# Last feed-forward of a four-layer network: tiles turned by DMA instead of TensorE, and both silus ahead of the older tile's rounding

## What is computed

```python
def _weight_quant(w):
    scale = 1.0 / jnp.clip(jnp.mean(jnp.abs(w)), 1e-05)
    wq = jnp.clip(jnp.round(w * scale), -1.0, 1.0) / scale
...
def _act_quant(x):
    scale = 127.0 / jnp.clip(jnp.max(jnp.abs(x), axis=-1, keepdims=True), 1e-05)
    xq = jnp.clip(jnp.round(x * scale), -128.0, 127.0) / scale
...
def _bitlinear(x, w):
    return jnp.einsum('bsi,oi->bso', _act_quant(x), _weight_quant(w))
gate = jax.nn.silu(_bitlinear(x, w_gate))
up = _bitlinear(x, w_up)
return _bitlinear(gate * up, w_down)
```

## Time and profile before

| | |
|---|---|
| time, 3 runs | 1109.73 us median, 1107.92 to 1112.27 |
| the profiled execution's own time | 1105.96 us |
| its span, first to last instruction | 1104.2 us |
| last feed-forward in the span | 992.7 to 1104.2 us |
| first matmul of its rounds | 1020.77 us |
| TensorE, VectorE, ScalarE, POOL busy over the span | 83%, 71%, 68%, 56% |
| mean granted TensorE clock | 0.934 |

### The profile page before, as it was taken

The page is one execution under the profiler, slowest core; times in us unless marked ns, Lnnn a source line. Parts: engine busy times, 40 slices in busy tenths (PEclk is TensorE's granted clock), DMA queues, the critical chain, the costliest instruction groups (busy, mean ns, idle before and its releaser), DMA issues. The chain is left out here.

```text
span 1104.2 us, 23943 instructions
## 1 busy us (share of the span) xinstructions
PE 914.9 (83%) x9014; PEld 698.9 (63%) x9014; DVE 782.2 (71%) x1550; ACT 745.7 (68%) x1254; POOL 623.5 (56%) x571
## 2 busy tenths in 40 slices
PE   5887998999999999997518999967888989960686
PEld 4655686767676777675417999955566767760344
DVE  5768778777877786676894444458978786639676
ACT  3387888698878887882533444445797878924686
POOL 2177766776686666772515555333686767813232
PEclk9899999999999999998758999988998999975899
DMA  9479999899989979994912222182899979943011
GB/s 265 164 127 193 160 157 152 153 171 151 163 145 184 158 149 152 149 175 65 321 67 73 77 75 75 58 282 43 173 187 173 168 145 172 173 78 114 6 35 39
DMA packets 433744, 153.57 MB, mean 139 GB/s; under 512 B 406592, under 2 KB 424192, under 8 KB 433600
## 3 DMA queue, kind: packets, MB, share of 16 engines
q1 hardware_dynamic: 429888, 141.82, 66.6%
q0 software_dynamic: 3744, 10.23, 2.9%
HBM read 38.62 MB, written 12.71 MB: 46 GB/s over the span
## 5 line engine op out<-in xcount | busy, mean ns | idle before, releaser
L477 POOL TENSOR_TENSOR A_PHL<-A_pr,A_PHL 128x508 f16<-128x508 f32 x256 | 295.2, 1159 | 134.5 <-ACT A_pr L754 133.6
L753 ACT ACTIVATE A_PHL<-A_ps,A_negmax 128x508 f16<-128x508 f32 x256 | 179.6, 701 | 17.9 <-DVE A_negmax L1003 15.3
L477 POOL TENSOR_TENSOR C_PHL<-C_pr,C_PHL 128x512 f16<-128x512 f32 x128 | 150.5, 1186 | 58.0 <-ACT C_pr L754 57.5
L754 ACT ACTIVATE A_pr<-A_ps,A_negmax 128x508 f32<-128x508 f32 x256 | 181.5, 709 | 0.0
L1003 DVE TENSOR_REDUCE A_negmax<-A_ps 128x2 f32<-128x1016 f32 x128 | 154.3, 1205 | 0.0
L598 PE MATMUL A_ps<-A_K,A_Q 64*128 64x512 f32 x768 | 124.1, 427 | 12.4 <-ACT A_pr L754 9.8
L616 PE MATMUL A_ps<-A_VH,A_PT 128*128 128x65 bf16 (+1 forms) x1024 | 109.5, 197 | 18.9 <-DMA A_PT<-A_PHL 18.6
L616 PEld LDWEIGHTS A_ps<-A_VH,A_PT 128*128 128x128 f16 (+1 forms) x1024 | 93.6, 98 | 47.7 <-DMA A_PT<-A_PHL 29.6
L617 PE MATMUL A_ps<-A_VL,A_PT 128*128 128x64 f16 (+1 forms) x1024 | 108.6, 194 | 0.0
L618 PE MATMUL A_ps<-A_VH,A_PT 128*128 128x65 bf16 (+1 forms) x1024 | 108.3, 195 | 0.0
L753 ACT ACTIVATE C_PHL<-C_ps,C_negmax 128x512 f16<-128x512 f32 x128 | 88.7, 693 | 15.1 <-DVE C_negmax L1003 14.5
(11 more groups left out here) (355 smaller groups left out, 2681.8 us busy)
## 6 DMA issues: line engine op xcount, KB each, us to landing
A_PT<-A_PHL SPq DMA_TRANSPOSE x256, 3.4
M_WINl<-in_L_ffn_w_in SPq DMA_DIRECT2D x4, 1024.0 KB, 11.9
M_WOUTl<-in_L_ffn_w_out SPq DMA_DIRECT2D x4, 1024.0 KB, 12.5
C_yc<-routed_rows SPq DMA_DIRECT2D x8, 512.0 KB, 5.2
ct_split<-A_CT SPq DMA_DIRECT2D x4, 768.0 KB, 4.1
C_CT<-ct_split SPq DMA_DIRECT2D x4, 768.0 KB, 8.0
M_rows<-M_xn SPq DMA_DIRECT2D x4, 512.0 KB, 9.0
out<-X SPq DMA_DIRECT2D x16, 128.0 KB, 1.7
```

The costliest lines, as they stand in the source:

```text
L477: pool.tensor_tensor(PHL[:, e % PRING, 1, 0:KEYS], pr[:, e % RING, 0:KEYS], PHL[:, e % PRING, 0, 0:KEYS], ALU.subtract).then_inc(pl_ready. ...
L753: a.activation(PHL[:, e % PRING, 0, 0:KEYS], o, ACT.Exp, bias=nm[:, n % 4, h:h + 1])
L754: a.activation(pr[:, e % RING, 0:KEYS], o, ACT.Exp, bias=nm[:, n % 4, h:h + 1]).then_inc(p_ready.sem, 1)
```

## The change

Input tiles and inner tiles are transposed by DMA, issued from SP, straight from SBUF to SBUF. TensorE's transposes and ScalarE's two copies go. The PSUM that they used becomes a third buffer of F_pg (GU = 3) and a second of F_py. F_xqT, F_hq and F_hqT get three buffers, and LAG, the rounds between a tile's start and its down product, goes from 3 to 4. On ScalarE silu(s, 1) moves ahead of h_round(s - 1). The three weight-load semaphores are shared with the attention's.

```diff
-    LAG = 3
+    LAG = 4
     XLEAD = 2
-    HB = 4
+    HB, HQ, XQ, GU = 4, 3, 3, 3
...
+            def turn_x(t):
+                sp.wait_ge(xq_ready, t // GRP + 1)
+                if t >= XQ:
+                    sp.wait_ge(gu_filled, 2 * (t - XQ + 1))
+                sp.dma_start_transpose(out=xqT[:, t % XQ, :, :], in_=xq[:, t // GRP % 2, t % GRP, :]).then_inc(xt_loaded[t % XQ], 16)
+
+            def turn_h(t):
+                sp.wait_ge(hq_ready, t + 1)
+                if t >= HQ:
+                    sp.wait_ge(y_filled, t - HQ + 1)
+                sp.dma_start_transpose(out=hqT[:, t % HQ, :, :], in_=hq[:, t % HQ, :]).then_inc(ht_loaded[t % HQ], 16)
+
+            def store(t):
                 sp.wait_ge(x_added, t + 1)
                 sp.dma_start(out[:, t, :], X[:, t, :]).then_inc(stored, 16)
+
+            for t in range(XLEAD):
+                turn_x(t)
+            for s in range(NT + LAG + 2):
+                if s + XLEAD < NT:
+                    turn_x(s + XLEAD)
+                if 2 <= s < NT + 2:
+                    turn_h(s - 2)
+                if s >= LAG + 2:
+                    store(s - LAG - 2)
...
             def gate_up(t, half):
                 u = 2 * t + half
                 if half == 0:
-                    pe.wait_ge(xt_copied, t + 1)
-                if u >= 2:
-                    pe.wait_ge(h_ready, u - 1)
+                    pe.wait_ge(xt_loaded[t % XQ], 16 * (t // XQ + 1))
+                if u >= GU:
+                    pe.wait_ge(h_ready, u - GU + 1)
...
+            def down(t):
+                pe.wait_ge(ht_loaded[t % HQ], 16 * (t // HQ + 1))
                 if t >= 2:
-                    pe.wait_ge(ht_copied, t - 1)
+                    pe.wait_ge(x_added, t - 1)
...
             for s in range(NT + LAG):
                 if s < NT:
                     silu(s, 0)
+                    silu(s, 1)
                 if 1 <= s <= NT:
                     h_round(s - 1)
-                if s < NT:
-                    silu(s, 1)
-                if LAG - 1 <= s < NT + LAG - 1:
-                    h_copy(s - LAG + 1)
-                if s + XLEAD < NT:
-                    x_copy(s + XLEAD)
```

More of the change, by code:

```diff
@@ L1638, in bit_ffn @@
         hs = sb("hs", [P, 2, H], F32)
-        hq = sb("hq", [P, 2, H], BF16)
-        hqT = sb("hqT", [P, 2, HC, P], BF16)
-        w_loaded = [sem(f"w_loaded{k}") for k in range(3)]
+        hq = sb("hq", [P, HQ, H], BF16)
+        hqT = sb("hqT", [P, HQ, HC, P], BF16)
+        w_loaded = [turn_of(stats, "attn", nc, f"w_{n}_loaded", 16) for n in "qkv"]
         chain_sem = sem("chain")
@@ L1654, in bit_ffn @@
         xq_ready = sem("xq_ready")
-        xt_filled = sem("xt_filled")
-        xt_copied = sem("xt_copied")
+        xt_loaded = [sem(f"xt_loaded{k}") for k in range(XQ)]
         gu_filled = sem("gu_filled")
@@ L1663, in bit_ffn @@
         hq_ready = sem("hq_ready")
-        ht_filled = sem("ht_filled")
-        ht_copied = sem("ht_copied")
+        ht_loaded = [sem(f"ht_loaded{k}") for k in range(HQ)]
         y_filled = sem("y_filled")
@@ L1685, in _ @@
             pe.wait_ge(sums_ready, 2)
[L1686 to L1695, removed]
+            mm(py[:, 0, 0:4], ones[:, :], wsum[:, :], start=True, stop=True).then_inc(sums_filled, 1)
             def gate_up(t, half):
@@ L1699, in gate_up @@
                 if half == 0:
-                    pe.wait_ge(xt_copied, t + 1)
-                if u >= 2:
-                    pe.wait_ge(h_ready, u - 1)
+                    pe.wait_ge(xt_loaded[t % XQ], 16 * (t // XQ + 1))
+                if u >= GU:
+                    pe.wait_ge(h_ready, u - GU + 1)
                 for j, W in enumerate((WG, WU)):
                     for kc in range(KC):
-                        last = mm(pg[:, half, j, :], xqT[:, t % 2, kc, :], W[:, kc, half * BANK:(half + 1) * BANK],
+                        last = mm(pg[:, u % GU, j, :], xqT[:, t % XQ, kc, :], W[:, kc, half * BANK:(half + 1) * BANK],
                                   start=(kc == 0), stop=(kc == KC - 1))
                 last.then_inc(gu_filled, 1)
-            def turn_h(t):
-                pe.wait_ge(hq_ready, t + 1)
+            def down(t):
+                pe.wait_ge(ht_loaded[t % HQ], 16 * (t // HQ + 1))
                 if t >= 2:
-                    pe.wait_ge(ht_copied, t - 1)
+                    pe.wait_ge(x_added, t - 1)
                 for c in range(HC):
[L1714 to L1722, removed]
+                    last = mm(py[:, t % 2, 0:D], hqT[:, t % HQ, c, :], WD[:, c, :], start=(c == 0), stop=(c == HC - 1))
                 last.then_inc(y_filled, 1)
-            for t in range(XLEAD):
-                turn_x(t)
             pe.wait_ge(w_ready, 3)
@@ L1749, in x_final @@
                 if g >= 2:
-                    pool.wait_ge(xt_filled, GRP * (g - 1))
+                    for t in range(GRP * (g - 2), GRP * (g - 1)):
+                        pool.wait_ge(xt_loaded[t % XQ], 16 * (t // XQ + 1))
                 pool.tensor_scalar(xq[:, g % 2, :, :], xr[:, g % 2, :, :], -MAGIC, 1.0, ALU.add, ALU.mult).then_inc(xq_ready, 1)
@@ L1784, in x_round @@
                              scale=xm[:, 1, t:t + 1]).then_inc(x_rounded, 1)
[L1786 to L1790, removed]
             for t in range(2 * GRP):
```

49 lines of the change are left out of this document (17 added, 32 removed).

## The result

The changed kernel takes 1095.35 us (median of 11 runs, 1091.27 to 1102.74), the kernel before, timed beside it, 1109.24 (11 runs, 1104.75 to 1113.45). The ratio is 0.988, with an interval of 0.9856 to 0.9904: 13.3 us less, give or take 2.7.

What follows compares the result with a forecast made beforehand. A closed 4.18 us loop through ScalarE and VectorE was taken as the bound, falling to 3.50. Loop -10.5 and end +1.9 gave -8.6 us: profiled 1105.96 to 1097.4, plus 3.8 for the median, 1101.1; range 1097.5 to 1106.0.

Steps and rivals of the forecast that it cites:

- rival 1: The forecast itself: VectorE paces the rounds; 1101.1 us, own range 1098 to 1104.5; chance 0.60.
- Gate to gate, 0.78: VectorE's round: second gate product 0.78 us after the first, part of 3.50 us a round (3.09 without an add).
- The collision, 1.2 us: VectorE's tensor_scalar waits for POOL's group rounding: 0.95 us in round 4, 0.25 in round 8; bounds 0 and 2.1.
- case 2: Larger gain through no collision, short landing and upper clock: 11.2 us, 1098.5 or somewhat less; chance 0.10.
- Moving the second silu is what breaks the loop; removing the transposes is worth nothing by itself.: ScalarE's second silu behind the previous tile's rounding closes the 4.18 us loop; copies and transposes are not on it.
- The end, +1.9: From the last marker to the span's end: 10.7 us in place of 8.8; bounds of the cost 0.5 and 6.0.
- SP: SP's issuing per round: 1.32 + 0.72 and a store, 3.4 us, upper 4.0, against 3.50; costed at nothing.
- The slack of the transposes: In mid-loop, input and inner transposes have over 4 us to spare, even at the 7.7 us maximum landing.
- 3: Long landing at the end, or late input transposes in the first rounds: up to 4.1 us more, 1105.2; chance 0.13.
- 4: Loop not really opened, TensorE's lead only three halves: at 0.5 us more a round, 1109; chance 0.07.
- 5: Transposes do not overlap in the loop: 6.7 us a round, +42 us, 1152; chance 0.05.
- 6: TensorE stays at its lower clock, 1.2 GHz: 5.3 us a round, +14 us, 1124; chance 0.05.

Runs made afterwards that it cites:

- e4: Changed kernel with the small tensor_scalar of each inner tile's scale over two columns in place of one; 1093.81 us, one run.
- e9: Changed kernel with input rounding one round later and scales of four tiles kept in groups of five columns; 1093.2 us, ratio 0.9873 against the kernel before.
- e2: Changed kernel with ScalarE's old order (silu, rounding, silu); 1110.64 us, ratio 1.0018 against the kernel before.
- e1: Kernel before with only both silus moved ahead of the older tile's rounding, TensorE still transposing; 1110.5 us, ratio 1.0019 against the kernel before.
- e7: Changed kernel with the add of the first 11 tiles moved from VectorE to ScalarE and POOL; 1093.59 us, ratio 0.9839 against the kernel before.
- e8: Changed kernel with input rounding one round later and the add of 11 tiles off VectorE; 1093.51 us, ratio 0.9855 against the kernel before.
- e10: Changed kernel with later input rounding, the add of 11 tiles off VectorE and five-column scale groups; 1091.78 us, ratio 0.9874 against the kernel before.
- e11: Changed kernel with later input rounding, the add of 11 tiles off VectorE and fewer scale instructions; 1090.1 us, ratio 0.9828 against the kernel before.
- e3: Changed kernel with two buffers of F_pg in place of three; 1098.42 us, ratio 0.9915 against the kernel before.
- e6: Changed kernel with each inner transpose issued as two DMAs of four blocks; 1106.4 us, ratio 0.9983 against the kernel before.

## Why the prediction was wrong

The sign and the pace-maker were right: VectorE paces the rounds, ScalarE and TensorE follow, nothing waits for a transpose in mid-loop, and the chain is the one of rival 1. The sizes were not: the loop gained 13.8 and not 10.5, and the end cost 1.3 and not 1.9, so the layer fell by 12.4 where I had 8.6. By itself that turns the forecast of 1101.1 into 1097.4, 0.1 below the range. The time, 1095.35, lies 2.15 below the range, and the other 2 us are in no term of mine: the kernel before was 0.5 us faster in 11 runs than in the 3 of the forecast, and 1.5 are within the 2.7 that the gain is uncertain by. Point by point:

**Gate to gate, 0.78 (the step that failed, with the next).** I took the spacing of two gates from the gate and the maximum behind it, since before a wait always parted two gates. Two in a row take 1.40 together (x2 at 1059.68), and the maximum starts 1.43 behind the first (1061.11), where I had charged 1.56. Rounds are 3.36, not 3.50, and 2.95, not 3.09; 15 x 0.14 = 2.1 us. The prediction should have had a bound below 0.78 here; no row of before shows two gates back to back, and I gave this term no range. A sign of it stood in the earlier trace rows. The maximum waits for the result of the gate ahead of it and starts 0.78 behind that gate's start, 0.03 after its 0.75 us are over. The gate behind the add needs nothing of it and starts 0.41 behind its start, 0.07 before its 0.48 us are over. I took the spacing of a pair in which the second waits for the first, and used it for two gates that do not wait for each other; the second of these starts some 0.66 behind the first (1.40 less 0.74), again 0.08 before the first is over. The rows agree with this reading throughout, but no run changes the waiting alone.

**The collision, 1.2 us (the other step that failed).** It did not happen: the 16 instructions L1868 took 0.15 each, the one inside POOL's instruction too. I had drawn the rule from one instruction of 2 columns and applied it to one of 1 column. e4 shows that with 2 columns it costs 0.58 in round 4 and 0.17 in round 8, 0.75 together, so that even there my 0.95 and 0.25 were too much. 2.1 + 1.2 = 3.3, which is the whole of 13.8 - 10.5. My case 2 had the missing collision, at a chance of 0.10, but not the faster gates, and 0 was a bound that I had written down myself, for another reason (a shift in phase).

By the runs, a tensor_scalar of one column is free and those of 2, 4 and 5 wait. I had expected 5 to be free, from 1 against 2 and 4; e9 says no (0.76). The Trainium skill, "VectorE: DVE Perf Modes", section "Mode 2×_2P — use both read ports for one tensor", lets a one-source operation take both read ports when its outermost dimension longer than one is even, or is the same for source and destination. I had read only the first half. With the second, 5 columns in place qualify and one column, which has no such dimension, does not: that rule, read whole, agrees with all four. That the second port is what VectorE waits for is not shown; the runs show only who waits.

**"Moving the second silu is what breaks the loop; removing the transposes is worth nothing by itself."** The second half holds (e2: 1.0018). The first does not: e1 has the move alone and gains nothing either, for a second loop of 4.43 us lies right behind the one of 4.18. I had found the loop that bounds the kernel and not asked which one comes next with the old transposes in place. The number did not suffer, since the change has both.

**The end, +1.9.** My terms add up to 10.6, not the 10.7 that I wrote, so it should have read +1.8. It was +1.3: the landing was 3.1, not 3.6, and the lower clock of the last down product came as worked out (1.89 against 1.87). That clock was a near thing: in e2, e4, e7, e8, e10 and e11 the product ran at the upper clock, 1.05 us, and the end is 0.5 longer than before, which is my lower bound. The runs do not show what decides between the two.

**SP.** The input transpose costs 1.18, not my 0.72; the upper bound, 1.32, was the nearer. The inner one is 1.25 (1.32), the store 0.57 (at most 1.32). What was wrong is the price per block that I had fitted from 8 and 16 blocks; between 2 and 8 blocks the rows differ by 0.07. The sum is 3.0, and 3.24 with the time between one DMA and the next, which I had left out. It stays below the round of 3.36, so that costing it at nothing held, but with 0.12 to spare, and by luck: 0.46 too little for the input transpose and 0.24 left out between the DMAs were made up by 0.75 too much for the store and 0.07 for the inner one. Rounds below 3.24, as in e7, live on the lead of the transposes, and a longer loop would use it up (argued from the two rounds, not run).

**The slack of the transposes.** I wrote that both have over 4 us to spare even at a landing of 7.7. By my own terms that landing leaves the input tile 14 - 1.6 - (2.40 + 1.3 + 7.7) = 1.0 us and the inner one 3.9. No harm came of it, since landings were at most 3.7 and 4.2.

**Start and the rounds with a group maximum.** The start was unchanged, as said (34.3 and 34.5). The two rounds are 6.01 and 5.94, where I had 3.04 + 3.09 = 6.13.

**Rivals.** 3: inner tiles landed in 3.1 us, 4.2 at most, so the end stayed short. 4: e3 takes a third of the lead away and steady rounds stay 3.36, so the lead was ample; only behind the stalls does it matter. 5: transposes overlap, as 3.36 us a round with landings of 2.3 and 3.1 shows; e6 shows where SP's queue does take over. 6: the clock is 1.00 in the steady part, and lower behind the stalls (3.16 us of idle time ahead of 1043.68, where two matmuls take 0.96) and at the end.

## What to carry to other kernels

A loop through several engines has a next-longest loop right behind it: undo each half of a change on its own before crediting one of them. A spacing of two instructions that never stood together in the trace is an unknown and needs bounds like any other; take it from a pair in which the second waits for the first only where that is so in the new order too. A queue's round is read from start to start: the durations of its DMAs alone came to 3.0 us, the round to 3.24. Where an engine has come to pace the rounds (97% busy), every small instruction on it counts in full: 0.4 us of an add (e7) and 0.9 and 1.4 us of small scale instructions (e11) came off the rounds that had them.

## What the runs showed of the hardware that I had not expected

- A transpose DMA costs SP about the same for 2, 4 and 8 blocks of 128x128: 1.18, 1.26 and 1.25 us; landings are 2.3, 2.5 and 3.1. The 16 blocks of the second attention cost 2.10, so this does not go on for ever. With the queue full, 0.05 to 0.10 us pass between two DMAs. The transposes also keep the DMA engines busy: 0.62 of the steady stretch at 134 GB/s, where the stores alone made 0.10 at 33.
- VectorE's tensor_scalar of one column runs through POOL's instruction (0.15), those of 2, 4 and 5 columns end with it (0.72, 0.76, 0.76). The reciprocal of 5 columns (0.19), the 1024-wide reduction and the gates also run beside POOL, the latter two at their usual 1.2 and 0.7. The runs do not show by themselves why one column differs.
- Two scalar_tensor_tensor of 128x512 in a row that do not wait for each other take 1.40 us, less than twice the 0.75 of one.
